# A graph kernel's last stage: centred weight and bias, z in PSUM, the own part laid under it by TensorE, stores from GpSimd

## The reference, cut to what matters

```python
def _L3_gnn_ref(h, W, b, alpha, gamma, beta, src, dst):
    h_neigh = jax.ops.segment_sum(h[src], dst, num_segments=N)
    deg = jax.ops.segment_sum(jnp.ones_like(dst, dtype=h.dtype), dst, num_segments=N)
    out = (h_neigh + h) / (deg + 1.0)[:, None]
    out = out @ W.T + b
    a = jax.nn.sigmoid(alpha)
    out = out * a + h * (1.0 - a)
    mu = jnp.mean(out, axis=-1, keepdims=True)
    var = jnp.var(out, axis=-1, keepdims=True)
    return (out - mu) * jax.lax.rsqrt(var + LN_EPS) * gamma + beta
# and around it
x = _layernorm(x + _L3_gnn_ref(x, ...), axis=-1)
```

## Time and profile before

| what | value |
|---|---|
| three runs | 5554.11, 5555.4, 5557.37 us; median 5555.4 |
| the profiled execution | 5562.63 us, its span 5560.8 us |
| first load of the last stage issued, last result made | 5039.5 us, 5547.4 us |
| busy over the span | PE 3402.8 us (61%), DVE 3821.4 (69%), ACT 2290.3 (41%), POOL 3010.4 (54%) |
| DMA moved | 1143.34 MB, mean 206 GB/s |

### The profile page before, as it was taken

One profiled execution on the slowest core, in us unless ns is written; L12 is line 12 of the kernel. 1 busy time (PEld: TensorE's weight loads), 2 busy tenths in 40 slices (PEclk: granted clock), 3 DMA queues, 4 the chain that ended last, 5 costly groups with the idle time before them and its releaser, 6 DMA issues. The chain is left out here.

```text
span 5560.8 us, 69536 instructions
## 1 busy us (share of the span) xinstructions
PE 3402.8 (61%) x19679; PEld 2644.3 (48%) x19679; DVE 3821.4 (69%) x11123; ACT 2290.3 (41%) x5289; POOL 3010.4 (54%) x2693
## 2 busy tenths in 40 slices
PE   5788844388513466631567635554999984774443
PEld 1455544377411355531466523333777763664443
DVE  8977767399644566521677677775888863666997
ACT  0344400299500355521223223333666652335776
POOL 7777777255567332277777547772455545550000
PEclk9999978699755799955788867777999997997665
DMA  4566588399667777631577357784566644785554
GB/s 193 161 186 182 176 297 274 105 302 312 212 201 254 262 251 248 228 96 52 153 249 234 115 148 256 253 260 148 199 218 209 212 166 149 244 254 190 208 208 156
DMA packets 694922, 1143.34 MB, mean 206 GB/s; under 512 B 109027, under 2 KB 451083, under 8 KB 688290
## 3 DMA queue, kind: packets, MB, share of 16 engines
q1 hardware_dynamic: 592748, 957.86, 51.9%
q0 software_dynamic: 101792, 181.03, 10.9%
HBM read 686.74 MB, written 463.45 MB: 207 GB/s over the span
## 5 line engine op out<-in xcount | busy, mean ns | idle before, releaser
L2258 PE MATMUL ro_end<-vals,end_mask 128*2 128x128 f32 x1600 | 240.0, 315 | 391.4 <-DVE vals L2122 286.1
L2381 POOL DMA_INDIRECT sc_rows<-layer,node_idx x392 | 385.5, 983 | 126.5 <-issue 119.1
L2906 POOL DMA_INDIRECT tf_edge_x<-y,tf_src_idx x196 | 193.1, 985 | 385.7 <-SPq L2882 332.9
L214 POOL DMA_INDIRECT x_src<-in_x_dram,node_idx x196 | 339.9, 1734 | 84.2 <-issue 58.4
L784 PE MATMUL msg_acc<-msg_pair,msg_vals 128*128 128x512 f32 (+3 forms) x392 | 208.3, 704 | 273.3 <-issue 241.7
L2258 PEld LDWEIGHTS ro_end<-vals,end_mask 128*2 128x2 f32 x1600 | 147.4, 96 | 475.7 <-DVE vals L2122 297.5
L3040 PE MATMUL tf_h_ps<-tf_x_t,pre_w 128*128 128x512 f32 x784 | 349.0, 598 | 20.4 <-ACT tf_hidden L3000 19.2
L1617 POOL DMA_INDIRECT cap_own<-layer,w_own x200 | 205.8, 1029 | 286.9 <-SPq L1597 234.9
L3000 ACT ACTIVATE tf_hidden<-tf_h_ps,pre_b 128x512 f32<-128x512 f32 x392 | 269.2, 687 | 221.8 <-PE tf_h_ps L3040 211.3
L3052 PE MATMUL tf_o_ps<-pre_w,tf_hidden 128*128 128x128 f32 (+1 forms) x3136 | 358.0, 275 | 0.0
L2284 PE MATMUL ro_acc<-vals,ro_mask 128*126 128x128 f32 x1600 | 243.1, 316 | 183.5 <-ACT ro_square L2216 140.4
(11 more groups left out here) (488 smaller groups left out, 10969.4 us busy)
## 6 DMA issues: line engine op xcount, KB each, us to landing
ro_mask<-masks SPq DMA_DIRECT2D x100, 504.0 KB, 4.3
layer<-zeros SPq DMA_DIRECT2D x96, 512.0 KB
si_both<-layer SPq DMA_DIRECT2D x48, 1024.0 KB, 6.3
ro_far<-far SPq DMA_DIRECT2D x75, 512.0 KB, 6.2
ro_both<-both SPq DMA_DIRECT2D x75, 512.0 KB, 6.0
agg<-zeros SPq DMA_DIRECT2D x48, 512.0 KB
mom_x<-in_x_dram SPq DMA_DIRECT2D x48, 512.0 KB, 9.4
mom_agg<-agg SPq DMA_DIRECT2D x48, 512.0 KB, 7.8
```

What stands on the lines that cost most here:

```text
L214: k.nc.gpsimd.indirect_dma_start(out=rows[:, t, :], out_offset=None, in_=k.x, in_offset=bass.IndirectOffsetOnAxis(ap=k.node_idx[:, 0, t:t ...
L2258: mm = nc.tensor.matmul(end_ps[0:2, j, :], k.end_mask[:, t, :], k.vals[:, t, :], start=True, stop=True, skip_group_check=True)
L2381: nc.gpsimd.indirect_dma_start(out=rows[:, g % SC, c * GT + j, :], out_offset=None, in_=k.layer1, in_offset=bass.IndirectOffsetOnAxis(ap=k ...
```

## The change

- In `Prepared.vector`, after the weight and the bias have been scaled, each has its mean over the 128 output features subtracted, row by row: a reduction, a scale by 1/128 and a subtraction, for each of the two tables. z then has mean zero, and its variance is the mean of its squares.
- z stays in PSUM, in three slots of two banks. TensorE first lays `own` into the two banks by two 128x512 matmuls with the identity, and the eight products accumulate on top of it. The product has lag 1 now and stands ahead of the transposes of the next unit; those write two banks that are used by every unit.
- ScalarE squares z from PSUM into SBUF (lag 1), VectorE sums the squares over the 128 features (`reduce`, lag 1) and adds the floor. The root is taken by ScalarE (lag 2) and inverted by VectorE (lag 2). The shift of the first normalisation is gone.
- The scaling of z is shared: nodes 0 to 3 of each partition by ScalarE (a Copy with a scale from a tile, out of PSUM, lag 3) and then gamma by VectorE on that half; nodes 4 to 7 by VectorE, scale and gamma in one operation out of PSUM (lag 3).
- The second normalisation is as before, but `scaled`, `total`, `res` and the small tiles have three slots instead of two, and its last part has lag 5.
- The stores are issued from GpSimd's queue; SP keeps the three loads.

The order of the parts in each engine's list changes with it. The diff:

```diff
@@ -1219,7 +1219,7 @@
         k.g2, k.be2, k.b2 = keep("g2", [P, 1]), keep("be2", [P, 1]), keep("b2", [P, D])
         k.cap_w, k.cap_b = keep("cap_w", [P, D]), keep("cap_b", [3, D])
         k.mean_wt, k.mean_bias, k.mean_beta = keep("mean_wt", [P, D]), keep("mean_bias", [P, D]), keep("mean_beta", [P, D])
...
+        k.mean_gamma, k.mean_mix, k.mean_floor = keep("mean_gamma", [P, D]), keep("mean_mix", [P, 6]), keep("mean_floor", [P, NCOL])
     def begin(self, inner):
         k, a = self.k, self.k.a
@@ -1274,7 +1274,7 @@
             .then_inc(self.exp, 1)
     def begin_vector(self, dve):
...
+        self.chain = Chain(dve, self.step, 63)
         self.chain.begin(0)
     def vector(self, n):
@@ -1296,6 +1296,10 @@
             c.link(v.tensor_scalar(mix[:, 3:4], mix[:, 2:3], -1.0, 1.0, ALU.mult, ALU.add))
             c.link(v.tensor_scalar(bias[:, :], bias[:, :], mix[:, 2:3], None, ALU.mult))
             c.link(v.tensor_scalar(k.mean_wt[:, :], self.w_ps[:, 0:D], mix[:, 2:3], None, ALU.mult))
+            for m, table in ((4, k.mean_wt), (5, bias)):
+                c.link(v.tensor_reduce(mix[:, m:m + 1], table[:, :], AX.X, ALU.add))
+                c.link(v.tensor_scalar(mix[:, m:m + 1], mix[:, m:m + 1], 1.0 / D, None, ALU.mult))
+                c.link(v.tensor_scalar(table[:, :], table[:, :], mix[:, m:m + 1], None, ALU.subtract))
         if n == 20:
             for out in k.qkv_parts + [k.bc_parts, k.bo_parts]:
                 ins = v.memset(out[:, :, :], 0.0)
@@ -3161,11 +3165,11 @@
 ML = 3
+MZ = 3
+MH = 4
 def mean_layer_phase(k, own_part, out):
     nc = k.nc
     with ExitStack() as st:
@@ -3173,10 +3177,14 @@
             return k.sb(st, "ml_" + name, shape)
         agg, own, shifted = (sb(x, [P, ML, NJ, D]) for x in ("agg", "own", "shifted"))
...
+        turned_sb, square = sb("turned_sb", [P, 2, NJ, P]), sb("square", [P, 2, NJ, D])
+        scaled, total, res = (sb(x, [P, ML, NJ, D]) for x in ("scaled", "total", "res"))
+        size, root, inv = (sb(x, [P, ML, NJ]) for x in ("size", "root", "inv"))
+        norm = Norm(k, st, "ml_norm", slots=ML)
+        turned_ps = [k.ps(st, f"ml_turned{b}", [P, 4, P]) for b in range(2)]
+        z = [[k.ps(st, f"ml_z{u}{b}", [P, 4, D]) for b in range(2)] for u in range(MZ)]
+        names = (["turned", "copied", "made", "squared", "reduced", "sized", "rooted", "inverted", "scaled_low", "scaled_high",
+                  "gained", "added", "res_made"] + [f"stored{u}" for u in range(ML)]
                  + [f"{x}_in{u}" for x in ("agg", "own", "shifted") for u in range(ML)])
         s = {x: k.sem(st, "ml_" + x) for x in names}
@@ -3194,91 +3202,142 @@
                         sp.dma_start(tile[0:p, u, :, :], node_rows(table, n, p)).then_inc(s[f"{what}_in{u}"], 16)
                     return stage
...
+                pipeline(NG + 1, (load(agg, k.agg, "agg", s["turned"]), 0), (load(own, k.own, "own", s["made"]), 0),
+                         (load(shifted, k.shifted, "shifted", s["added"]), 2))
+            @block.gpsimd
+            def _(pool):
+                for n in range(NG + 1):
+                    pool.wait_ge(s["res_made"], n + 1)
+                    nc.gpsimd.dma_start(node_rows(out, n, tail(n)), res[0:tail(n), n % ML, :, :])\
+                        .then_inc(s[f"stored{n % ML}"], 16)
+                for n in range(NG + 1 - ML, NG + 1):
+                    pool.wait_ge(s[f"stored{n % ML}"], nth(n))
             @block.vector
             def _(dve):
                 v = nc.vector
...
+                norm.prepare(dve)
+                def reduce(n):
+                    u, p = n % ML, tail(n)
+                    dve.wait_ge(s["squared"], n + 1)
+                    v.tensor_reduce(size[0:p, u, :], square[0:p, n % 2, :, :], AX.X, ALU.add).then_inc(s["reduced"], 1)
+                    dve.wait_ge(s["reduced"], n + 1)
+                    v.scalar_tensor_tensor(size[0:p, u, :], size[0:p, u, :], 1.0 / D,
+                                           own_part.floor[0:p, n * NJ:n * NJ + NJ], ALU.mult,
+                                           ALU.add).then_inc(s["sized"], 1)
+                def invert(n):
+                    u, p = n % ML, tail(n)
+                    dve.wait_ge(s["rooted"], n + 1)
+                    v.reciprocal(inv[0:p, u, :], root[0:p, u, :]).then_inc(s["inverted"], 1)
+                def high(n):
+                    u, p = n % ML, tail(n)
+                    dve.wait_ge(s["inverted"], n + 1)
+                    for j in range(MH, NJ):
+                        ins = v.scalar_tensor_tensor(scaled[0:p, u, j, :], z[n % MZ][j // 4][0:p, j % 4, :],
+                                                     inv[0:p, u, j:j + 1], own_part.gamma[0:p, :], ALU.mult, ALU.mult)
+                    ins.then_inc(s["scaled_high"], 1)
+                def low(n):
+                    u, p = n % ML, tail(n)
+                    dve.wait_ge(s["scaled_low"], n + 1)
+                    v.tensor_tensor(scaled[0:p, u, 0:MH, :], scaled[0:p, u, 0:MH, :],
+                                    own_part.gamma[0:p, :].unsqueeze(1).broadcast_to([p, MH, D]),
                                     ALU.mult).then_inc(s["gained"], 1)
                 def add(n):
...
+                    u, p = n % ML, tail(n)
+                    dve.wait_ge(s[f"shifted_in{u}"], nth(n))
+                    dve.wait_ge(s["scaled_high"], n + 1)
                     dve.wait_ge(s["gained"], n + 1)
...
+                    if n >= ML:
+                        dve.wait_ge(s["res_made"], n - ML + 1)
+                    v.tensor_tensor(total[0:p, u, :, :], scaled[0:p, u, :, :], shifted[0:p, u, :, :],
                                     ALU.add).then_inc(s["added"], 1)
                     dve.wait_ge(s["added"], n + 1)
...
+                    norm.statistics(dve, n, u, p, total[:, u, :, :])
+                pipeline(NG + 1, (invert, 2), (lambda n: norm.negate(dve, n, n % ML, tail(n)), 4), (high, 3), (low, 3), (add, 3),
+                         (reduce, 1))
             @block.scalar
             def _(act):
...
+                def copy(n):
+                    p = tail(n)
+                    act.wait_ge(s["turned"], n + 1)
                     if n >= 2:
...
+                        act.wait_ge(s["made"], n - 1)
+                    for b in range(2):
+                        ins = nc.scalar.activation(turned_sb[:, n % 2, 4 * b:4 * b + 4, 0:p], turned_ps[b][:, :, 0:p],
+                                                   ACT.Copy)
+                    ins.then_inc(s["copied"], 1)
+                def square_up(n):
+                    p = tail(n)
+                    act.wait_ge(s["made"], n + 1)
+                    if n >= 2:
+                        act.wait_ge(s["reduced"], n - 1)
+                    for b in range(2):
+                        ins = nc.scalar.activation(square[0:p, n % 2, 4 * b:4 * b + 4, :], z[n % MZ][b][0:p, :, :], ACT.Square)
+                    ins.then_inc(s["squared"], 1)
+                def take_root(n):
+                    u, p = n % ML, tail(n)
+                    act.wait_ge(s["sized"], n + 1)
+                    nc.scalar.activation(root[0:p, u, :], size[0:p, u, :], ACT.Sqrt).then_inc(s["rooted"], 1)
+                def scale(n):
+                    u, p = n % ML, tail(n)
+                    act.wait_ge(s["inverted"], n + 1)
+                    if n >= ML:
+                        act.wait_ge(s["added"], n - ML + 1)
+                    for j in range(MH):
+                        ins = nc.scalar.activation(scaled[0:p, u, j, :], z[n % MZ][j // 4][0:p, j % 4, :], ACT.Copy,
+                                                   scale=inv[0:p, u, j:j + 1])
+                    ins.then_inc(s["scaled_low"], 1)
                 def finish(n):
...
+                    u, p = n % ML, tail(n)
+                    if n >= ML:
+                        act.wait_ge(s[f"stored{u}"], nth(n - ML))
+                    norm.normalise_on_act(act, n, u, p, res[:, u, :, :], total[:, u, :, :]).then_inc(s["res_made"], 1)
+                pipeline(NG + 1, (take_root, 2), (lambda n: norm.square_root(act, n, n % ML, tail(n)), 4), (scale, 3),
+                         (finish, 5), (copy, 0), (square_up, 1))
             @block.tensor
             def _(pe):
...
                 def turn(n):
+                    p = tail(n)
                     pe.wait_ge(s[f"agg_in{n % ML}"], nth(n))
...
+                    if n:
+                        pe.wait_ge(s["copied"], n)
+                    for j in range(NJ):
+                        mm = nc.tensor.transpose(turned_ps[j // 4][:, j % 4, 0:p], agg[0:p, n % ML, j, :], k.ident[0:p, 0:p])
+                    mm.then_inc(s["turned"], 1)
+                def product(n):
+                    p = tail(n)
+                    pe.wait_ge(s[f"own_in{n % ML}"], nth(n))
+                    if n >= MZ:
+                        pe.wait_ge(s["scaled_low"], n - MZ + 1)
+                        pe.wait_ge(s["scaled_high"], n - MZ + 1)
```

(41 more changed lines are left out.)

36 lines of the change are left out of this document (removed).

## The result

The changed kernel took 5465.67 us (median of four runs, 5460.19 to 5471.12), the kernel before beside it 5556.39: a ratio of 0.9831, interval 0.9818 to 0.9845. 5474 was forecast, 5456 to 5525 the range. The profiled execution took 5464.26 us, its span 5462.5, against 5562.63 and 5560.8: 98.3 us of span are gone. The medians lie 90.7 apart: the profiled execution before took 6.2 us more than its median, the one after 1.4 less.

A forecast was written before the change was run, and what follows sets the result against it. VectorE's own sum was taken to bound the old 10.03 us step, ScalarE's run plus the reduction the new 8.2. Fill, 44 steps and drain saved 84 us, less 2 for the last store and 1 for links: 5474, range 5456 to 5525.

The forecast's parts named there:

- the hand-over: Last stage, step border: reduction waits for ScalarE's squares, next root waits for the reduction; step 6.76 + 1.44 = 8.2 us.
- the four scales: ScalarE's run in a last-stage step: four Copy operations with a scale take 1.17 us, upper bound 1.54.
- the gamma multiply: VectorE's run in a last-stage step: gamma on the lower half takes 0.63 us.
- the fill: Start of the last stage, through step 4: first transposes end at 5045.1, step 4 at 5075.5; 36.0 us.
- the drain: End of the last stage: three VectorE steps, then ScalarE's root and two finishes, 5436.3 to 5463.4; 27.1 us.
- The last store: Kernel's end: only the last store from GpSimd is bare, costing 2 us, bounds 0 and 5.
- The six links: Early stage: six small operations added on VectorE cost 1 us, at most 1.6, or vanish behind its loads.
- TensorE is not the bound: Rival, last stage: TensorE bounds at the low clock, 9.4 us a step, 5527 at worst; chance 0.16.
- The ring of result tiles: Rival, last stage: GpSimd stores over 21 us make finish wait; slower kernel from 27 us a store; chance 0.05.
- The transfers: Rival, last stage: 2.1 MB a step at 209 GB/s keeps the step at 10.0, time 5555; chance 0.05.
- longer runs: Rival, last stage: ScalarE's or VectorE's run exceeds its rows, step 8.6 to 9.0, 5492 to 5509; chance 0.10.
- the largest wait of VectorE: Sign in the last stage: VectorE's largest wait would be the reduction waiting for ScalarE's squares, 0.35 us a step.

The follow-up runs named there:

- VectorE's statistics shorter: Changed kernel with seven instead of eight of VectorE's statistics instructions in a unit: 5457.48 us, ratio 0.9829 to the kernel before, step 7.92 us.
- own laid twice: Changed kernel with TensorE laying the own part under z twice, result unchanged: 5457.96 us, ratio 0.9830 to the kernel before, step 8.02 us.
- both are shortened: Changed kernel without one of ScalarE's eight last normalising activations and one of VectorE's eight statistics instructions: 5446.28 us, ratio 0.9804, step 7.84 us.
- the order alone: Changed kernel reordered only, squares and their reduction ahead of the total's addition and statistics: 5437.66 us beside 5463.42 for the changed kernel, step 7.36 us.
- the multiply moved to GpSimd: Reordered changed kernel (squares and reduction earlier), with the lower half's gamma multiply on GpSimd instead of VectorE: 5437.31 us, ratio 0.9786, step 7.57 us.
- squares earlier: Changed kernel reordered only, ScalarE squaring before the last normalisation and VectorE reducing before the total's addition: 5438.75 us, again 5437.66, step 7.36 us.
- own on VectorE: Changed kernel with VectorE adding own in PSUM again and TensorE's laying taken out: 5506.46 us, ratio 0.9907 to the kernel before, step 8.92 us.

## Why the prediction was right, and where not

The time was right, 5474 for 5465.67; the sum of its terms was nearly right; the reason given for the largest term was wrong, and that the term still came within 0.17 us a step was luck.

**The step.** "The step is ScalarE's run plus the reduction, 6.76 + 1.44 = 8.2 us", was the forecast. This step of the argument failed: ScalarE's run is 6.41 to 6.44, so the hand-over would make 7.9 and stands, as the step does with VectorE's statistics shorter, behind VectorE's own 8.03. Two terms were mis-sized. ScalarE: the first root starts 0.03 behind the size and the second 0.12 behind the first (I had 0.29 for both), and the four scales take 1.00 to the next start, not 1.17. VectorE: 7.85 was forecast, and its stretch for the inversions (0.79 for 0.8), scale-and-gain (1.03 for 1.07), add and statistics (3.90 for 3.75 + 0.15) and reduction (1.42 for 1.44) came as written; the gamma multiply came as 0.89 to the next start instead of 0.63. It was priced by its duration, and the add that needs its result right behind it waits 0.20 more. In the earlier trace rows the gamma multiply had other work behind it, the add of own, and so no such wait. The two misses, 0.3 too much on one engine and 0.2 too little on the other, changed which engine ends last and hardly the step: with ScalarE alone sized right, the same argument would have given 7.9, hardly above VectorE's forecast 7.85.

**The parts of the stage.** 44 steps of 8.03 (5071.34 to 5424.52) are 353.2 instead of 360.8, the fill 34.4 instead of 36.0, the drain 27.8 instead of 27.1: 415.4, 8.5 less than forecast, 7.6 of it the steps'. In the fill, the first laying of own took 3.1, where the sum has 3.5 without a row. The last store cost 3.2 less and not 2 more: it had been sized from the medians of the earlier trace rows, which are those of full units, and for the last unit they do not hold (10.4 from SP, 3.4 from GpSimd). The six links took 1.7 us of VectorE (808.04 to 809.76; 1.6 was the bound) and lengthened nothing: the products of the moments stage, first to last, span 226.0 us, before 226.1.

**The rivals.** TensorE is not the bound: with own laid under z it never idles for more than 1.7 between 5100 and 5350, its clock stays at 1.00, and own and product take 1.96 and 2.05 where the product alone took 3.76 behind 4.58 idle. That was argued and came; with own laid twice it still had time. The ring of result tiles was never waited for: the stores' median landing is 6.0 against 21 of slack, and their issue took GpSimd 0.54 on the mean of 49, so none was held up; by the rule that the prediction weighed (the Trainium skill, "SBUF — State Buffer", "Who interferes with whom") with no more than an 8-column tensor_scalar in the step the sum was to stay, and the trace agrees. The transfers did not pace: 264 GB/s, and between 5100 and 5350 nothing waits for a load; behind the fill only TensorE does, at the last unit. A step of 8.6 to 9.0 from longer runs did not come. As to what would show it: I had written that the largest wait of VectorE would be the reduction waiting for the squares; there is one in 31 steps. That line showed the error before any experiment did.

## What to carry to other kernels

When two engines hand over to each other in every step, sum both of them from start to start, each with the waits for what was just issued, on its own engine too; if the sums lie within a few per cent, shortening one can give nothing or half, as here, and only a run in which both are shortened shows that. An operation that leaves a full engine is worth its time less what it had been covering: here the add's 0.89 of 1.28. Before moving work to another engine, look for waits on something just issued and put independent work into them: the order alone gave 26 us of kernel time, the multiply moved to GpSimd nothing. And look at the last, partial unit by itself: here its load of own took 22 us, where a full unit's took 4.5.

## What the runs showed of the hardware

- A dependent VectorE operation right behind a 128x512 multiply waited 0.20 for its result; an independent one began 0.08 before the multiply's record ended (5199.49 against 5198.89 + 0.68).
- In these runs TensorE's granted clock went with the length of its gaps and not with the amount of its work: 1.00 with 121 or 160 busy us of 200 and gaps of up to 1.7, 0.91 with 142 busy us and gaps of up to 3.2 (squares earlier), 0.69 with gaps of 4.0 on the mean (own on VectorE).
- The last unit's store of 106 partitions took 10.4 us from SP's queue, at a DMA share of 0.11, and 3.4 from GpSimd's, at 0.46; the end of the kernel lay 13.4 and 10.2 us behind the issue.
- A two-input 8-column operation of VectorE grew from 0.17 to 1.02 us beside GpSimd's multiply.
